# A gated cross-attention and expert block: the second tile prepared earlier, through banks that expert work uses later

## What is computed

```python
x = x + tanh(g_xattn) * xattn(layernorm(x), ctx)
x = x + tanh(g_ffn) * ffn(layernorm(x))

def xattn(x, xf):                       # 16 heads of 8
    xn, xfn = layer_norm(x) * g + b, layer_norm(xf) * tg + tb
    q, k, v = xn @ Wq + bq, xfn @ Wk + bk, xfn @ Wv + bv
    return softmax(q k^T / sqrt(8)) v   # 128 queries, 77 keys, per head

def ffn(x):                             # 8 experts, the best 2 of them per row
    logits = x @ w_router
    h = square(relu(x @ w1[e]))         # for every expert e
    return sum over the top 2 of softmax(top logits)[e] * (h[e] @ w2[e])
```

## Time and profile before

| | |
|---|---|
| median of 3 runs | 312.18 us |
| profiled execution | 316.11 us |
| span in it | 314.3 us |
| mean granted TensorE clock in it | 0.978 |
| busy: TensorE, VectorE, ScalarE, GpSimd | 292.4, 232.0, 179.3, 112.6 us |
| chain that ended last: TensorE, VectorE, issue, ScalarE, DMA, GpSimd | 57, 26, 7, 4, 4, 2% |

### The profile page before, as it was taken

How to read it: one execution, slowest core, us unless ns; L and a number is a source line. 1 busy time by engine, 2 the same in 40 slices (tenths; PEclk the granted TensorE clock), 3 DMA queues, 4 the chain that set the end, 5 groups by cost and what they waited for, 6 DMA issues and landing times.

```text
span 314.3 us, 7841 instructions
## 1 busy us (share of the span) xinstructions
PE 292.4 (93%) x2837; PEld 240.6 (77%) x2837; DVE 232.0 (74%) x934; ACT 179.3 (57%) x412; POOL 112.6 (36%) x211
## 2 busy tenths in 40 slices
PE   7987899799999999999999999999999889989994
PEld 5555586577878888888888888888788778778784
DVE  7887677757779885988688868886668656646665
ACT  0524566535665666566665676566656555555473
POOL 6593552562126621661266126422512211221110
PEclk9999989958999999999999999999999999999999
DMA  3361301282439535652657264816392620080011
GB/s 71 94 159 56 63 6 51 49 120 55 154 124 111 101 119 194 111 104 74 234 98 115 78 237 66 103 45 232 81 113 47 194 81 3 6 293 9 2 35 33
DMA packets 18070, 30.83 MB, mean 98 GB/s; under 512 B 5209, under 2 KB 11514, under 8 KB 18032
## 3 DMA queue, kind: packets, MB, share of 16 engines
q1 hardware_dynamic: 11136, 22.35, 29.6%
q0 software_dynamic: 3408, 6.61, 9.1%
q10 hardware_dynamic: 3488, 1.38, 1.7%
HBM read 18.94 MB, written 2.21 MB: 67 GB/s over the span
## 4 chain that ended last, share of the span: by engine, by line
PE 57%; DVE 26%; issue 7%; ACT 4%; DMA 4%; POOL 2%; DVEq 0%; POOLq 0%; ACTq 0%
PE y L595 13%; PE c L550 9%; PE ab L506 6%; DVE u L1157 4%; PE s L527 4%; DVE negm L1040 3%; PE ab L573 3%; DMA gb<-gates_scratch 3%; PE ab L565 2%; PE h L461 2%; PE h L588 2%; PE ab L456 2%; PE h L590 2%; PE h L589 2%; DVE o L1063 2%
## 5 line engine op out<-in xcount | busy, mean ns | idle before, releaser
L1040 DVE TENSOR_REDUCE negm<-ab 128x4 f32<-128x308 f32 x128 | 60.5, 476 | 38.5 <-PE ab L506 36.6
L821 ACT ACTIVATE p<-s 77x512 f32<-77x512 f32 x128 | 74.5, 584 | 18.1 <-PE s L527 17.9
L527 PEld LDWEIGHTS s<-qs,ks 104*77 104x77 f32 x512 | 55.8, 153 | 12.3 <-issue 4.2
L527 PE MATMUL s<-qs,ks 104*77 104x128 f32 x512 | 61.2, 243 | 0.8 <-ACT p L821 0.8
L595 PE MATMUL y<-w2s,hs 128*128 128x128 f32 x448 | 60.4, 279 | 1.4 <-ACT hs L826 1.2
L595 PEld LDWEIGHTS y<-w2s,hs 128*128 128x128 f32 x448 | 55.4, 193 | 3.4 <-ACT hs L826 2.5
L1385 POOL TENSOR_SCALAR rs<-mv 128x1 f32<-128x1 f32 x32 | 7.3, 228 | 133.2 <-DVE mv L1079 133.2
L506 PE MATMUL ab<-ks,qs 96*128 96x312 f32 x128 | 50.2, 393 | 4.4 <-DVE negm L1040 1.5
L826 ACT ACTIVATE hs<-u 128x512 f32<-128x512 f32 x56 | 35.0, 624 | 14.1 <-DVE u L1157 14.1
L1157 DVE SCALAR_TENSOR_TENSOR u<-h,gb 128x512 f32<-128x512 f32 x56 | 38.0, 678 | 3.6 <-DMA gb<-gates_scratch 2.0
L550 PE MATMUL c<-p,vs 77*32 77x128 f32 x1024 | 35.4, 280 | 0.0
(11 more groups left out here) (128 smaller groups left out, 507.5 us busy)
## 6 DMA issues: line engine op xcount, KB each, us to landing
gb<-gates_scratch SPq DMA_DIRECT2D x14, 768.0 KB, 5.9
gb<-gates_scratch SPq DMA_DIRECT2D x7, 512.0 KB, 3.7
qs<-q_hi SPq DMA_DIRECT2D x12, 256.0 KB, 7.3
out_dram<-y_out POOLq DMA_DIRECT2D x7, 256.0 KB, 6.2
x_sb<-in_x_dram POOLq DMA_DIRECT2D x6, 256.0 KB, 3.6
qs<-q_lo SPq DMA_DIRECT2D x6, 256.0 KB, 9.0
ks<-k_hi SPq DMA_DIRECT2D x34, 39.0 KB
ks<-k_lo POOLq DMA_DIRECT2D x32, 39.0 KB, 3.2
```

The lines of the kernel that those rows point to most:

```text
L527: mm = nc.tensor.matmul(p[0:N, T * i:T * i + T], ks[:, par, c, i, NP * j:NP * j + N], qs[:, par, c, T * j:T * j + T], start=True, stop=True)
L821: nc.scalar.activation(p32[:, m % LR, :], src, ACT.Exp).then_inc(p_done, 1)
L1040: nc.vector.tensor_reduce(negm[:, :, c], bank_ab[bank][:, 0:J * NP].rearrange("t (i n) -> t i n", n=NP)[:, :, 0:N], AX.X, ALU.max, negate= ...
```

## The change

- Uses of the preparation of tiles 1 and 2, and the values of tile 0, leave the order of the two banks. `SIDE` gives each a bank of the experts or of the values (2 is `h_0`, 3 `h_1`, 4 `y`, 5 `c`) and its turn in it.
- Tile 1: its context is turned in slot (-1, 1), its `x` in (-1, 2), keys are projected in (-1, 2), and queries in (-1, 3). Its queries take `project_queries`, with a copy by SyncE, one by ScalarE (`stack_q_rows`) and the low one by SyncE. Tile 2 has its second high copy issued by ScalarE too.
- The rows of keys of tile 0 are split over three queues instead of two (`stack_first_k`), those of tile 1 are shared otherwise between SyncE and GpSimd.
- `vs` is cleared by ScalarE in slots (-1, 1) and (-1, 3), with the ones set by GpSimd (`mark_values`); three of eight pieces of `ks` of tile 1 are cleared by ScalarE at the start, five by GpSimd, three of them at the start.
- `w2` is loaded in slot (0, 0). ScalarE prepares `w1` in (-1, 2) and `w2` in (0, 2) and (0, 3); VectorE makes the low part of `w1` in (0, 0).
- `values` go first in slots (0, 2) to (1, 1). In slot (0, 1), the first transposed scores of the next batch go ahead of the next tile's scores, and the second normalisation ahead of its first maximum. The fillers change banks, and two of (-1, 3) go.
- The second half of `bq` is loaded by SyncE, and tile 1's context and `x` ahead of `Wv`.

```diff
-AB_MOVED = [(("k", 0), ("ctxT", 0)), (("ctxT", 1), ("mT1", 0)), (("xT", 1), ("s1b2", 0)), (("k", 1), ("s1d2", 0))]
+AB_MOVED = [(("k", 0), ("ctxT", 0))]
+SIDE = {("v", 0): (5, 1), ("ctxT", 1): (2, 1), ("xT", 1): (3, 1), ("k", 1): (4, 1), ("q", 1): (2, 2),
+        ("ctxT", 2): (2, 3), ("xT", 2): (3, 2), ("k", 2): (4, 2), ("q", 2): (2, 4)}
 
 
 def ab_sequence(tiles):
 
     uses = [(name, step + shift) for step in range(-2, tiles + 1) for shift, name in AB_USES
-            if 0 <= step + shift < tiles and (name, step + shift) not in (("q", 0), ("q", 1))]
+            if 0 <= step + shift < tiles and (name, step + shift) != ("q", 0)
+            and (name, step + shift) not in SIDE]
...
-        CONSTS, ONES, WEIGHTS = 11, 3, 3
+        CONSTS, ONES, WEIGHTS = 11, (3, 4), 3
         CTX_WEIGHTS, X_WEIGHTS, ZEROED = 3, 3, (2, 2 * NC)
-        PREPARING = ((0, 1), (0, 2), (0, 3), (1, 0))
+        PREPARING = {(0, 2): (2,), (0, 3): (3,)}
         NG, NB_, BQ, BK, TG, TB, GX, GF, BQS = range(9)
 
...
-        bank_ab = [ps("ab_0"), ps("ab_1")]
+        bank_ab = [ps("ab_0"), ps("ab_1"), bank_h[0], bank_h[1], bank_y, bank_c]
...
+            if (name, s) in SIDE:
+                return SIDE[name, s]
...
-                turned = third if j == (3 if i == -1 else 2) else None
-                made = (1, 1) if (i, j) == (0, 0) else third if j == 3 and i != -1 else None
+                turned = third if j == 2 and i != -1 else None
+                made = third if j == 3 and i != -1 else None
...
-            return 2 if s == 0 else J
+            return {0: 0, 1: J - 1}.get(s, J)
...
-                        if term == 2 and i < k_shared(s):
+                        if term == 2 and (i < k_shared(s) or (s == 0 and i > 0)):
...
                 for term in ((0, 1), (2,))[a]:
+                    if term == 1 and s < 3:
+                        continue
...
+            for i in range(J // 2, J):
+                with nc.allow_non_contiguous_dma(reason="short vectors"):
+                    sp.dma_start(vec[QROWS * i:QROWS * i + QROWS, BQ:BQ + 1],
+                                 bq[QROWS * i:QROWS * i + QROWS].rearrange("(g d o) -> d g o", d=HD,
+                                                                           o=1)).then_inc(bq_in, 16)
+            sp.dma_start(ctx_sb[:, 1], ctx_v[1]).then_inc(ctx_first[1], 16)
+            sp.dma_start(x_sb[:, 1], x_v[1]).then_inc(x_first[1], 16)
             for dst, src in ((wv[0:L, :], Wv), (wv[L:L + 1, :], bv.rearrange("(o n) -> o n", o=1))):
...
+                    if (i, j) == (-1, 2):
+                        stack_k(1, 1)
                     if (i, j) == (-1, 3):
+                        stack_q(1, 1, 0)
+                        stack_q(1, 1, 1)
+                    if (i, j) == (0, 0):
                         unit_rows(1)
 
...
+                    pe.wait_ge(q_rows_made, 1)
...
-                    values_first = i == S - 1 and j > 1
+                    values_first = (i == S - 1 and j > 1) or (i == 0 and j > 1) or (i == 1 and j < 2)
...
+                    if (i, j) == (-1, 2):
+                        project_keys(1)
...
-                        (project_queries if made[0] >= 2 else project_query_rows)(made[0])
+                        (project_queries if made[0] else project_query_rows)(made[0])
...
+                    if (i, j) == (0, 1):
+                        scoresT(*near[1], 0)
                     if near[3]:
                         scores(*near[3], 0)
-                    if (i, j) == (-1, 3):
-                        keep_on(bank_s2[1], 2)
-                    if near[1]:
+                    if near[1] and (i, j) not in ((-1, 3), (0, 1)):
...
+                    if (i, j) == (-1, 1):
+                        transpose_ctx(1)
+                    if (i, j) == (-1, 2):
+                        transpose_x(1)
+                    if (i, j) == (-1, 3):
+                        scoresT(*near[1], 0)
...
+            def stack_first_k():
+
+                act.wait_ge(zeroed[0], ZEROED[0])
+                act.wait_ge(hi_k, 1)
+                for i in range(1, J):
+                    r = 2 * QROWS + HD * i
+                    act.dma_start(ks[r:r + HD, 0, :, i, :].bitcast(F32),
+                                  k_hi[QROWS * i:QROWS * i + QROWS].rearrange("p b n -> p (b n)").bitcast(F32))\
+                        .then_inc(k_stacked[0], 16)
...
+            def stack_q_rows(s, par):
+
+                if s >= 2:
+                    act.wait_ge(s2_ready, NC * G * (s - 1))
+                act.wait_ge(hi_q, s)
+                act.dma_start(qs[QROWS:2 * QROWS, par].bitcast(F32), q_hi[:, :].bitcast(F32))\
+                    .then_inc(q_stacked[par], 16)
+
+            def clear_some(par, some):
+
+                nc.scalar.activation(vs[:, par, some].rearrange("n b h v -> n (b h v)")
+                                     .rearrange("n (o k) -> n o k", k=D),
+                                     ident[0:N, :].rearrange("n (o k) -> n o k", o=1)
+                                     .broadcast_to([N, (some.stop - some.start) * H * VT // D, D]),
+                                     ACT.Copy, scale=0.0).then_inc(v_ones[par], 1)
+
...
+            act.wait_ge(const_made, 2)
+            for c, half in ((2, 1), (3, 0), (3, 1)):
+                nc.scalar.activation(ks[:, 1, c, 2 * half:2 * half + 2].rearrange("p i n -> p (i n)")
+                                     .rearrange("p (o k) -> p o k", k=MR),
+                                     ident[0:MR, 0:MR].rearrange("p (o k) -> p o k", o=1)
+                                     .broadcast_to([MR, 2 * G * NP // MR, MR]),
+                                     ACT.Copy, scale=0.0).then_inc(zeroed[1], 1)
...
-                        load_experts()
+                        load_experts(w1_in[:, :, :], w1.rearrange("e c d -> c e d"), first_in)
+                    if (i, j) == (-1, 1):
+                        clear_some(0, slice(0, G))
+                        evacuate_v(0, 0)
+                        evacuate_ctxT(1)
+                        clear_some(1, slice(0, G // 2))
+                        continue
+                    if (i, j) == (-1, 2):
+                        evacuate_k(1, 1)
+                        max_store(*near[2])
+                        evacuate_xT(1)
+                        prepare_experts(0)
+                        prepare_experts(1)
+                        continue
+                    if (i, j) == (-1, 3):
+                        max_store(*near[2])
+                        evacuate_q(1, 1)
+                        stack_q_rows(1, 1)
+                        clear_some(1, slice(G // 2, G))
+                        exponent(*near[1], 0)
+                        continue
...
+                    if made and made[0] == 0:
+                        stack_first_k()
...
-                        (evacuate_q if made[0] >= 2 else split_query_rows)(*made)
+                        (evacuate_q if made[0] else split_query_rows)(*made)
...
+                    if made and made[0] == 2:
+                        stack_q_rows(*made)
...
-                    if (i, j) in PREPARING:
-                        prepare_experts(PREPARING.index((i, j)))
+                    for part in PREPARING.get((i, j), ()):
+                        prepare_experts(part)
+                    if (i, j) == (0, 0):
+                        load_experts(w2s[:, :, :], w2.rearrange("e d c -> d e c"), experts_in)
...
-                        ahead = prepare
+                        ahead = prepare if i > 0 else none
...
-                    if (i, j) == (0, 3):
-                        ahead = low_experts()
                     if made:
-                        prepare = chained(low_keys(*made), (low_queries if made[0] >= 2 else low_query_rows)(*made))
+                        prepare = chained(low_keys(*made), (low_queries if made[0] else low_query_rows)(*made))
+                    if (i, j) == (0, 0):
+                        prepare = chained(low_queries(1, 1), low_experts())
                     if (i, j) == (-2, 3):
                         take(prepare)
...
-                        clear_values(dve, nc.vector, 0)
...
+                    if (i, j) == (-1, 1):
+                        take(normalise_ctx(1, 1), 2)
+                    if (i, j) == (-1, 2):
+                        normed = normalise_x(1, 1)
+                        take(top_scores)
+                        take(normed)
+                        take(top_scores, 4)
+                        take(normed)
+                        take(tops_of(near[3]))
+                        take(low_keys(1, 1))
...
+                    if (i, j) == (0, 1):
+                        normalise2(*near[-1])
                     if near[3] and (j != 2 or i <= 0):
                         take(tops_of(near[3]))
-                    if near[-1] and (j < 2 or (j == 2 and i < S - 1) or (j == 3 and i == S - 1)):
```

(38 more changed lines are left out.)

67 lines of the change are left out of this document (31 added, 36 removed).

## The result

| | before | after |
|---|---|---|
| median | 312.73 us (13 runs) | 316.19 us (13 runs) |
| profiled execution | 316.11 us | 313.2 us |
| span in it | 314.3 us | 311.4 us |
| mean granted clock in it | 0.978 | 0.980 |

The ratio of the times, after to before, is 1.0081 with a 95% interval of [1.0054, 1.0108]: slower by 0.8%, and outside the range forecast. Runs over 1.5% above a kernel's fastest are classed as slow and left out of every ratio. The two profiles say the opposite, and neither is typical. The one of after is its shortest run (the others: 314.9 to 318.4 us at mean clocks of 0.962 to 0.973). That of before is a long one: in the comparison that ran beside the first experiments, 17 of its 24 runs have 0.991 to 1.000 and 311.65 to 312.77 us. So the profiles are read for the order of events, the ratios for the verdict.

The account below looks back on a forecast made before the run. TensorE was taken to bound the kernel, with only the front, up to slot (1, 2), able to shift. Savings of 0.5 + 2.3 + 2.6 - 1.5 + 1.9 = 5.8 us from 312.18 gave 306.4 us, range 302.0 to 309.8.

Parts of the forecast that it names:

- Up to slot (0, 0), 0.5 saved: Before slot (0, 0): VectorE's 1.76 us clearing goes, half the gain eaten by the keys' part; 0.5 us saved.
- Slot (0, 0), 2.3 saved: Slot (0, 0): tile 1's row-wise projection leaves it, so 4.2 us for 6.46; 2.3 us saved.
- the sum: All parts of the front added, 0.5 + 2.3 + 2.6 - 1.5 + 1.9: 5.8 us saved.
- Slot (0, 1), the wait of 1.5 us: End of slot (0, 1): TensorE waits 0 to 3.2 us for tile 1's query copy, taken as 1.5 us lost.
- 2.6 less 1.5: Slot (0, 1): 6.4 us for 9.04, so 2.6 us saved, and 1.5 us lost waiting for tile 1's queries.
- Slot (0, 2), nothing: Slot (0, 2): TensorE is busy 6.64 of 6.97 us at full clock, so nothing saved.
- the 0.68 named for `w2`'s half: Slot (0, 2): ScalarE's half of `w2` costs one instruction, 0.68 us, if TensorE's work no longer covers it.
- Slot (0, 3), 1.9 saved: Slot (0, 3): three bank waits for tile 2's preparation go, so 7.4 us for 9.33; 1.9 us saved.
- Slots (1, 0) and (1, 1), nothing for the median: Slots (1, 0) and (1, 1): timed runs mostly lack the half clock, so nothing counted for the median.
- The 3.5 forecast for the profile alone: Slots (1, 0) and (1, 1): with full clock in place of the half clock, 3.5 us saved in a profile.
- The fourth rival: Slot (0, 1), tile 1's first score: the query wait takes the clock down, early slots save nothing; 315.9 us, chance 0.07.

Follow-up runs that it names:

- the first experiments: The earliest follow-up runs, from e1_rows on, timed beside the kernel before.
- e10_held_loads: Changed kernel with high query copies by SyncE only, tile 1's copies held until batch 1's maxima rows land, tile 2's loads and `w2` early; ratio 0.9861 to before.
- e4_tile2: Kernel before with only tile 2's preparation moved to the expert banks, fillers in other banks; ratio 0.9972 to the kernel before.
- e1_rows: Changed kernel with tile 1's queries projected row by row again in slot (0, 0), without DMA copies; ratio 1.0063 to the kernel before.
- e2_loads: Changed kernel with tile 2's loads and `w2` issued in slot (-1, 0); ratio 1.0117 to the kernel before.
- e9_two: Kernel before with only tile 2's second high query copy issued by ScalarE; ratio 0.9998 to the kernel before.
- e6_one2: Changed kernel with tile 2's high query copies both issued by SyncE, tile 1 as in the change; ratio 0.9979 to the kernel before.
- e16_order_held: e10_held_loads with tile 1's query copies behind batch 2's maxima rows on SyncE, held until those are in; ratio 0.9876 to the kernel before.
- e8_held: Changed kernel with high query copies by SyncE only, tile 1's copies held until batch 1's turned maxima land; ratio 0.9903 to the kernel before.
- e13_short: e10_held_loads with four fillers in slot (0, 0), ahead of the scores waiting for batch 1's maxima; ratio 0.9960 to the kernel before.
- e14_short2: e13_short with five more fillers in slot (1, 1), ahead of tile 2's first score; ratio 0.9967 to the kernel before.
- e3_fill: Changed kernel with eleven fillers in slot (0, 0), ahead of the scores waiting for batch 1's maxima; ratio 1.0162 to the kernel before.
- e15_order: e10_held_loads with tile 1's query copies issued behind batch 2's maxima rows on SyncE, with no hold; ratio 0.9874 to the kernel before.
- e17_order_fill: e15_order with four fillers in slot (0, 0); ratio 0.9946 to the kernel before.
- e12_all: e8_held with tile 2's loads and `w2` early and batch 1's maxima rows issued by ScalarE; ratio 0.9906 to the kernel before.

## Why the prediction failed

*Up to slot (0, 0), 0.5 saved.* Right, more or less: the slot opens at 27.74 us for 28.58. The first low query rows are written at 14.97 for 16.27, a wait of 1.19 us for `ks<-k_hi` before 19.66 gives some back, and tile 1's low query part and batch 2's rows go out at 30.35 and 30.98, as reckoned ("near 30.4"). ScalarE's clearings are priced now: 1.90 us for 2048 columns and 1.04 for 1024, near VectorE's 1.76 and the 0.9 for a half that the prediction took. One table load was made, of 1.28 us.

*Slot (0, 0), 2.3 saved.* Failed in the changed kernel, near right without most of the copies' harm. The first head should have been near 33 us and is at 39.64; in e10_held_loads it is at 34.48, 2.5 us ahead of before. There the slot runs from 28.54 to about 33.0, 4.5 us with a wait of 1.22 in it, where the sum has 4.2.

*Slot (0, 1), the wait of 1.5 us. **This is the step that failed**, in place, kind and size.* "What comes late next is the copy of tile 1's queries": the copies were taken as something that TensorE waits for, at tile 1's first score, and each was priced by landings of copies issued one behind the other by SyncE. What the copies do to others was left out. Their own landings were taken too short as well, 10.3 us at most: the low copy took 12.1 and was in at 42.4 us, and `w2` took 14.0 where 5.5 were counted. TensorE, held up before, got to tile 1's first score at 44.66 and no longer noticed. In the changed kernel the wait is 5.07 us, a slot earlier, for a transfer of 16 KB that the diff doesn't touch, and another 1.62 us in (1, 1), for tile 2's keys. The prediction's own rule, that every DMA of a moved step counts with the queues it passes, was applied to what stands behind SyncE's wait, not to what shares the DMA engines. Their share was to be had: 0.85 in slot (1, 0), where tile 2's copies cross, against 0.20 in (0, 0). The net of this slot, 2.6 less 1.5, did come between the heads of the profile (7.60 us for 9.03), but by luck: with no wait for a query copy, and with the clock at half up to 42 us.

*Slot (0, 2), nothing.* 7.80 us between heads for 7.37, at full clock. The 0.4 us more are within the 0.68 named for `w2`'s half if its cover goes; no run here tells whether they are that.

*Slot (0, 3), 1.9 saved.* Right: 7.04 us between heads for 8.78, and no wait for `xnT`, `k_lo` or `q_lo`. e4_tile2 shows that in the timed runs it gave 0.28% [-0.03, 0.58], some 0.9 us.

*Slots (1, 0) and (1, 1), nothing for the median.* Half right. The median of before has indeed hardly any half clock: in the first comparison its runs of 0.999 and 1.000 took 311.65 to 312.52 us (but for one of 528.35) and those of 0.987 to 0.989 took 313.15 to 314.18. But the same was assumed of the changed kernel, and none of its 13 runs is above 0.980. At a like clock it is the faster one: 313.2 us at 0.980, against 315.30 to 316.08 for eight runs of before at 0.982 to 0.984. By these the schedule saved some 2.5 us. That is an estimate and flatters the change, since some of its half clock falls into the stand of 32 to 36 us, where nothing runs. That the stands took more than this by way of the clock is argued, not shown: which stretches are slow in the typical runs of after no trace shows, since the one profiled is its fastest. The nearest to it are e1_rows and e2_loads, which keep the two queues for tile 2; in both the clock is down behind the wait for `k_hi`, and in the trace of after it is not.

The 3.5 forecast for the profile alone did come: the half clock of slot (1, 0) is gone, and there are 6.73 us between its heads for 10.44. That one slot gives 3.7 us, more than the 3.0 by which the two profiles differ at the head of (1, 3); the rest of the front lost 0.7.

The fourth rival had the mechanism (a wait for a DMA into `qs` brings the clock down) and, by chance of its terms, the time (315.9 for 316.19), with a chance of 0.07. Its place and its transfer were wrong, and its condition, a landing after 39.5, was met (42.4) without deciding anything. The sum of the other terms looks better in e10_held_loads. Six of seven runs of e10_held_loads have 308.75 to 309.32 us at 0.983 to 0.988; beside them, seven of the kernel before at 0.982 to 0.988 have 314.01 to 315.82. Between the two medians are 5.6 us, where the sum says 5.8. But median against median over all runs the gain is 4.0, and in the one trace, which is of its longest run (312.85 us), the lead over before is 2.5, 2.3, 1.9 and 3.7 us at the first four heads, where the sum comes to 5.8 by the fourth. So the sum isn't borne out term by term: slot (0, 1) gave nothing there, and the match of the totals is in part luck.

## To carry to other kernels

Price a large copy by what it does to the small transfers in flight beside it: list who is waited for while it crosses, and give those the landing time of the large one. An earlier schedule also spends slack that transfers had; a second queue that was free before (e9_two) cost 1% after it (e6_one2 against the changed kernel). And before clearing a half clock with fillers, look at which transfer the slow work is waiting beside: where it lands last, full clock only turns work into standing.

## What the hardware showed

- One transfer of 16 KB within SBUF took 2.05 us when nothing large was in flight (batch 2's rows in e16_order_held), 3.82 with `k_hi` rows ahead of it (e10_held_loads), 5.06 with the loads of tile 2 and `w2` beside it as well (e8_held), 6.26 behind three query copies in its queue, 7.34 with a copy of 256 KB issued by another engine in the same instant and others behind it (e2_loads), and 8.49 with both these copies and the loads. The Trainium skill (DMA: Bandwidth & Descriptors, Queues, rings and completion order) says that the increment of a semaphore lands only after every earlier write of its DMA engine, across that engine's queues. The trace fits this, with 8.49 us for rows that left in the same instant as ScalarE's copy, but no run here tells it from plain sharing of the engines. The same page (Issuing engines are not separate DMA queues) says that a second issuing engine saves only the time of issue. e9_two agrees: the ScalarE copy lands after 4.6 us, the copies and rows of keys behind it later than in before, and the time is the same.
- Fillers inside a stand held the granted clock at 1.00 in one trace (30 to 40 us in e13_short) and not in another (0.72 and 0.50 from 30 to 34 us in e14_short2, with the same four there). In e10_held_loads the two stands (1.22 us before 32.44, 1.58 us before 70.22) were followed by a clock of 0.50 from 34 to 40 and from 72 to 78 us. It cost nothing the first time, since a transfer took as long. Behind the wait for tile 2's rows in slot (1, 1) the clock fell in all four traces whose wait was 1.77 us or more (e2_loads, e3_fill, e15_order, e17_order_fill) and in none of the six with 0.66 to 1.39 us; at 1.56 to 1.64 us it fell in two of five (in e1_rows and e10_held_loads, not in after, e12_all and e13_short). These are counts of single traces, not a rule.
- The mean clock differs between kernels as well as between runs of one: 0.978 to 1.000 before, 0.962 to 0.980 after, 0.977 to 0.988 in e10_held_loads.
- That the half clock behind 32 us costs nothing in every run of e10_held_loads is inferred from one trace, that of its longest run; and a version with the query copies both early and out of the way of the maxima rows was not found.
